# Splitting keys and queries on GpSimd, transposing attention sums on VectorE in 32 by 32 blocks, and padding earlier, in a fused attention and expert kernel

## What is computed

```python
scores = jnp.clip(jnp.einsum('bhqd,bhkd->bhqk', Q, K), -80.0, 80.0)
scores = jnp.where(causal, scores, -jnp.inf)
weights = jax.nn.softmax(scores / jnp.sqrt(jnp.float32(d_qk)), axis=-1)
attn = jnp.einsum('bhqk,bhkd->bhqd', weights, V)
x = _layernorm(x + attn.transpose(0, 2, 1, 3).reshape(B, S, 128) @ W_O)
top_idx = jnp.argmax(x @ gate_w.T + gate_b + expert_bias, axis=-1)
# out += (top_idx == e) * (relu(x @ w1[e] + b1[e]) @ w2[e] + b2[e])   for each expert e
x = _layernorm(x + out)
```

## Time and profile before

| | us |
|---|---|
| median of 3 runs | 439.85 (438.35 to 442.32) |
| the profiled execution | 439.83 |
| its span (first to last instruction) | 438.1 |
| mean granted TensorE clock | 0.982 of full |

### The profile page before, as it was taken

The page is one execution under the profiler, slowest core; times in us unless marked ns, Lnnn a source line. Parts: engine busy times, 40 slices in busy tenths (PEclk is TensorE's granted clock), DMA queues, the critical chain, the costliest instruction groups (busy, mean ns, idle before and its releaser), DMA issues. The chain is left out here.

```text
span 438.1 us, 12324 instructions
## 1 busy us (share of the span) xinstructions
PE 416.3 (95%) x4235; PEld 230.2 (53%) x4235; DVE 362.1 (83%) x824; ACT 356.4 (81%) x568; POOL 152.1 (35%) x164
## 2 busy tenths in 40 slices
PE   8899999999999999999999999998999899699993
PEld 6533344444443444444444444443444698599992
DVE  3978897999998889999987999999878578377764
ACT  3979999999998999998899999998889564376661
POOL 8221001315213013512401314212001466688887
PEclk9889999999999999999999999999899999899998
DMA  5268510668671135544500760674410255477640
GB/s 154 50 167 195 162 49 1 144 145 227 145 170 30 45 87 126 123 112 103 133 2 6 164 149 27 142 170 133 125 39 2 73 140 156 146 223 197 200 136 20
DMA packets 33005, 50.62 MB, mean 116 GB/s; under 512 B 5627, under 2 KB 16545, under 8 KB 32944
## 3 DMA queue, kind: packets, MB, share of 16 engines
q1 hardware_dynamic: 25488, 36.51, 34.1%
q10 hardware_dynamic: 5184, 9.05, 7.3%
q0 software_dynamic: 2272, 4.27, 2.9%
HBM read 21.35 MB, written 5.33 MB: 61 GB/s over the span
## 5 line engine op out<-in xcount | busy, mean ns | idle before, releaser
L1032 ACT ACTIVATE prob<-ring 128x1024 f32<-128x1024 f32 x288 | 274.5, 1039 | 25.8 <-PE ring L1224 25.0
L1242 PE MATMUL o_acc<-prob,v_stat 128*32 128x512 f32 (+3 forms) x1536 | 155.8, 501 | 2.9 <-DVE prob L705 2.1
L1224 PE MATMUL ring<-queries,keys 32*128 32x512 f32 (+3 forms) x1536 | 126.8, 385 | 0.4 <-DVE queries L665 0.4
L1224 PEld LDWEIGHTS ring<-queries,keys 32*128 32x128 f32 x1536 | 71.0, 187 | 71.4 <-issue 48.0
L691 DVE TENSOR_SCALAR prob<-prob 128x2048 f32<-128x2048 f32 x64 | 77.4, 1220 | 7.2 <-ACT prob L1032 6.8
L705 DVE SCALAR_TENSOR_TENSOR prob<-prob,mask_hi 128x1024 f32<-128x1024 f32 (+1 forms) x80 | 82.2, 1028 | 0.0
L1120 ACT ACTIVATE prob<-ring,b1T 128x128 f32<-128x128 f32 x156 | 44.6, 368 | 35.6 <-issue 16.4
L704 DVE TENSOR_SCALAR prob<-prob 128x1024 f32<-128x1024 f32 (+1 forms) x80 | 64.7, 808 | 6.6 <-ACT prob L1032 6.1
L584 POOL DMA_INDIRECT by_expert<-xrow,index x32 | 40.1, 1254 | 78.1 <-DVE index L800 71.0
L1242 PEld LDWEIGHTS o_acc<-prob,v_stat 128*32 128x32 f32 x1536 | 34.1, 109 | 57.2 <-issue 39.5
L565 POOL TENSOR_TENSOR rstd<-var_eps,const 128x4 f32<-128x4 f32 x8 | 16.4, 2048 | 92.0 <-DVE var_eps L748 92.0
(11 more groups left out here) (117 smaller groups left out, 343.5 us busy)
## 6 DMA issues: line engine op xcount, KB each, us to landing
queries<-query_parts SPq DMA_DIRECT2D x60, 256.0 KB, 4.0
v_stat<-in_w ACTq DMA_DIRECT2D x34, 256.0 KB
keys<-key_parts SPq DMA_DIRECT2D x60, 128.0 KB, 2.5
queries<-by_expert SPq DMA_DIRECT2D x39, 66.0 KB
xrow<-in_x_rows SPq DMA_DIRECT2D x8, 264.0 KB, 4.4
xT<-in_x_T SPq DMA_DIRECT2D x8, 256.0 KB, 3.0
v_stat<-in_w SPq DMA_DIRECT2D x5, 256.0 KB
out<-prob,queries POOLq DMA_INDIRECT x39
```

What stands on the lines that cost most here:

```text
L1032: act.activation(prob[u % P_SLOTS][:, 2 * half:2 * half + 2, :].rearrange("p h s -> p (h s)"), slot(("score", u, half))[:], ACT.Exp, scale ...
L1224: last = pe.matmul(out[:, j % 2 * QC + off:j % 2 * QC + off + w], keys[hg][r, kt * P:(kt + 1) * P], queries[hg][r, qc, part, QC - w:QC], s ...
L1242: last = pe.matmul(o_acc[j * VW:(j + 1) * VW, QC - w:QC], v_stat[b % 2][:, hg, kt, j, :], prob[u % P_SLOTS][:, j, off:off + w], start=begi ...
```

## The change

Four things are done together.

1. **GpSimd makes the lower parts.** `lower_of_keys` and `lower_of_queries` leave VectorE; `parts_of` on GpSimd runs the two casts and then the two subtractions. Project jobs of the own batch's second pair move from units 3 and 8 to 10 and 13.
2. **Sums are turned by VectorE.** The jobs "turn" and "flip" are gone from TensorE, and the flip's evacuation from ScalarE. VectorE transposes `o_sb` in 32 by 32 blocks (`turn_sum`), takes one reciprocal and one product per sum, and, for the second pair, transposes again (`attn_turned`). W_O's rows are reordered on loading to match. This happens right behind the clip of the unit in which ScalarE copies the sum (n = 7, 20, 25 and 2 of the next batch).
3. **Pads in the last batch.** SyncE lays 1152 padding rows (the most that the last batch and a tile can need) behind each region straight from DRAM to DRAM, eight DMAs of 608 KB, before the last batch's routes write over them. Those routes wait for `padded`. No pad is left in the expert loop.
4. **The early plan in four parts**, at units 23, 24, 27 and 28 of the last batch, and the tail's late jobs and plan one tile earlier.

```diff
-OWN_JOBS = {3: ("project", 1, 0), 8: ("project", 1, 1),
-            16: ("turn", 0, 0), 23: ("turn", 0, 1), 26: ("turn", 1, 0), 28: ("flip", 0), 29: ("out", 0),
-            33: ("turnx", 0), 34: ("gate", 0), 35: ("rank", 0)}
-LATE_JOBS = {4: ("turn", 1, 1), 6: ("flip", 1), 7: ("out", 1), 10: ("turnx", 1), 12: ("gate", 1), 14: ("rank", 1)}
-NEXT_JOBS = {18: ("latent", 0), 20: ("latent", 1), 24: ("v", 0), 25: ("project", 0, 0), 30: ("v", 1), 31: ("project", 0, 1)}
+OWN_JOBS = {10: ("project", 1, 0), 13: ("project", 1, 1), 29: ("out", 0), 33: ("turnx", 0), 34: ("gate", 0),
+            35: ("rank", 0)}
+LATE_JOBS = {7: ("out", 1), 11: ("turnx", 1), 12: ("gate", 1), 14: ("rank", 1)}
+NEXT_JOBS = {20: ("latent", 0), 25: ("latent", 1), 26: ("project", 0, 0), 27: ("v", 0), 30: ("v", 1),
+             31: ("project", 0, 1)}
-TAIL_AT = {1: "turn", 2: "flip", 3: "out", 6: "turnx", 7: "gate", 8: "rank"}
-PLAN_AT = (8, 9, 10)
-EARLY_PLAN_AT = (B - 1) * UB + 16
-ROUTE_AT = {9: (0, 1), 10: (2, 3)}
-PAD_AT = 9
-PADS_ACT = 2
+TAIL_AT = {2: "out", 5: "turnx", 6: "gate", 7: "rank"}
+PLAN_AT = (7, 8, 9)
+EARLY_PLAN_AT = (23, 24, 27, 28)
+ROUTE_AT = {8: (0, 1), 9: (2, 3)}
+PAD_ROWS = S + P
...
+                    for q in range(Q):
+                        sp.wait_ge(routed[q], b * QT * 16)
+                    sp.wait_ge(pad_ready, 1)
+                    for e in range(E):
+                        at = sp.value_load(pad_at[0:1, e:e + 1], min_val=0, max_val=DUMMY - PAD_ROWS)
+                        sp.dma_start(by_expert[bass.ds(at, PAD_ROWS), :], io["pad_rows"]).then_inc(padded, 16)
...
-            pad(sp, range(E - PADS_ACT))
...
+                pool.wait_ge(upper_keys, i + 1)
+                pool.tensor_tensor(key_parts[i % 2][:, 1, :], whole_k[i % 2][:], key_parts[i % 2][:, 0, :], ALU.subtract
+                                   ).then_inc(lower_keys, 1)
+                pool.wait_ge(upper_queries, i + 1)
+                pool.tensor_tensor(query_parts[i % 2][:, 1, :], whole_q[i % 2][:], query_parts[i % 2][:, 0, :], ALU.subtract
+                                   ).then_inc(lower_queries, 1)
...
+            def turn_sum(k):
+                dve.wait_ge(o_out, k + 1)
+                dve.transpose(flipped[k % NQC][:], o_sb[k % 2][:]).then_inc(o_turned, 1)
...
             def normalize(k):
...
+                dve.reciprocal(rsum[:], o[:, :, DH:2 * VS:VS]).then_inc(rsum_ready, 1)
                 dve.wait_ge(rsum_ready, k + 1)
...
+                if pair == PAIRS - 1:
+                    dve.wait_ge(attn_ready, k + 1)
+                    dve.transpose(flipped[qc][:], attn_blocks[qc][:]).then_inc(attn_turned, 1)
```

More of the change, by code:

```diff
@@ L96, in numbered @@
     kind, *which = job
-    if kind == "turn":
-        return kind, sums(b, *which)
     return (kind, b, *which) if kind in ("project", "direct") else (kind, b * NQC + which[0])
@@ L364, in taken @@
             i = which[0]
-            return {"turn": (attn_ready, i + 1), "flip": (flip_out, i + 1), "out": (added, i + 1),
+            return {"out": (added, i + 1),
                     "turnx": (turnx_out, i + 1), "gate": (logits_out, i + 1), "rank": (carried, i + 2),
@@ L590, in _ @@
                 if step_job(u, "project"):
[L591 removed]
+                    parts_of(*step_job(u, "project")[1:])
                 if route_at(u):
@@ L802, in job @@
             def job(kind, i):
-                if kind == "turn":
-                    normalize(i)
                 if kind == "out":
@@ L821, in before_clip @@
                     turn_queries(*which)
-                if kind == "turn":
-                    normalize(*which)
                 if kind == "out":
@@ L896, in _ @@
                 clip(u)
-                split = 0 if u == 0 else u - 1 if u > 1 else None
-                if split is not None and step_job(split, "project"):
-                    lower_of_keys(*step_job(split, "project")[1:])
-                    lower_of_queries(*step_job(split, "project")[1:])
+                if sum_ended(u) is not None:
+                    turn_sum(sum_ended(u))
                 if u == 20:
@@ L1257, in job @@
                 claim_misc((kind, i))
[L1258 to L1271 removed]
+                if kind == "out":
+                    pe.wait_ge(attn_turned, i + 1)
                     pe.wait_ge(out_w_in, 16)
@@ L1435, in key_query_weights, with output_weights @@
     return out
+def output_weights(a):
+    rows = a["L0_attn_W_O"].reshape(PAIRS, 2, HG, DH, D).transpose(2, 0, 1, 3, 4)
+    return np.ascontiguousarray(rows.reshape(HEADS * DH, D))
 def constants():
```

195 lines of the change are left out of this document (81 added, 114 removed).

## The result

The changed kernel takes **455.9 us** (median of 4 runs, 453.91 to 466.43) against 440.97 us of the kernel before beside it (438.35 to 442.32): a ratio of 1.0344, 95% interval 1.0291 to 1.0397. It is slower by 3.4%, where the prediction had 427 us and a range up to 441. One of the four runs, 466.43 us, was slow as a whole (clock 0.83 where the others have 0.96 to 0.97), and the ratio is made without it; the other three took 453.91 to 456.30 us.

The account below looks back on a forecast made before the run. TensorE was taken as the bound, VectorE and ScalarE at 92% right behind. 438.1 - 6.0 + 1.0 - 3.0 - 4.0 - 1.0 = 425.1 us of span, forecast 427 us, range 418 to 441.

Parts of the forecast that it names:

- part 3: Attention batches: GpSimd's subtractions, 1.2 us each, would hold VectorE 0.9 us in three of four cases, 5.4 us a batch.
- the period: Inner batch: VectorE's need of 78.5 us beside TensorE's 77.7, plus 2 us, gives 80.5 us; -6.0 us over 3.93 batches.
- rival (a): Attention batches: every subtraction holds a clip 1.0 us, VectorE needs 81.1 and becomes the bound; 437 us, chance 0.18.
- Rival (b): Attention batches: subtractions of 1.8 us each hold VectorE 1.6 us, its need 85.9, period 87; 452 us, chance 0.12.
- Parts 1 and 2: Attention batch: turns and flips gone save TensorE 3.5 us and ScalarE 1.3; VectorE's own work falls 2.1 us.
- the places: Project jobs moved within a batch: 1 to 2 us to spare for the longer chain, nothing booked.
- The start: First batch: keys just spread come later by about one subtraction, +1.0 us.
- Part 4: Last batch: the early plan in four parts removes 2.1 us of idle TensorE and 1.7 of clock; -3.0 booked.
- Part 5: Expert loop: pads moved out recover most of 5.5 us lost there, -4.0 booked; in the last batch they just fit.
- Part 6: Tail: its turn and flip leave TensorE, 2 x 0.65 us, and VectorE gains some 2 us; -1.0 booked.

Follow-up runs that it names:

- e1: The changed kernel with the lower parts of keys and queries made by VectorE again, GpSimd's subtractions gone: 431.5 us, 0.9834 of the kernel before.
- e3: The kernel before, with GpSimd also doing each lower-part subtraction (512 columns) into unread scratch while VectorE makes the real ones: 459.08 us, 1.0438.
- e10: The kernel before, with two more GpSimd casts of 128x512 per project into unread scratch: 440.96 us, 1.0056.
- e13: The kernel before, with two more GpSimd subtractions of 256 columns per project into unread scratch: 443.19 us, 1.0084.
- e15: The changed kernel with each GpSimd subtraction of 512 columns issued as two of 256: 443.38 us, 1.0083 of the kernel before.
- e8: e1 with the jobs back at the places of the kernel before: 437.58 us, 0.9955 of the kernel before.
- e7: e1 with the early plan in one piece at unit 16 of the last batch, as before: 431.85 us, 0.9836 of the kernel before.
- e14: The kernel before with only the early plan split in four, at units 18, 20, 22 and 24 of the last batch: 437.14 us, 0.9943.
- e6: e1 with the pads back in the expert loop, issued by SyncE and ScalarE, none in the last batch: 430.76 us, 0.9807 of the kernel before.
- e16: The changed kernel with GpSimd's subtractions halved and the next batch's second-keys project at unit 28 instead of 31: 453.99 us, 1.0300 of the kernel before.
- e2: The kernel before with only the lower parts moved to GpSimd, in its old order of jobs: 452.67 us, 1.0316.
- e4: The changed kernel with the next batch's second-keys project at unit 28 instead of 31: 444.33 us, 1.0109 of the kernel before.
- e5: e1 with the eight last routes spread, one behind each of tiles 1 to 4 and 8 to 11: 438.93 us, 0.9984 of the kernel before.

## Why the prediction was wrong, point by point

"Part" is here a part of the prediction. GpSimd's subtractions, point 1 of the change, are its part 3.

**The step that failed is part 3**, and with it the period. "A subtraction would cost 1.2 - 0.18 = 1.0 ... I take 0.9" was close for one meeting (1.08). "Not each one will meet a clip ... I take three in four" gave 5.4 us a batch, and that was too little: e1's VectorE shows 77.5 us, of which 5.4 are its own subtractions, so 72.1 without them, and the changed kernel shows 80.6 and 81.8. That is 8.5 and 9.7 us of waits, as if every subtraction held it for 1.1 to 1.2 us. VectorE's need was near the 81.1 of rival (a). Then "with two within a microsecond of each other ... I add 2 us: 80.5". This is what fell hardest. The batches took 85.8 and 88.7, so 5 to 7 us over VectorE's busy time. Adding up an engine's busy time treats a wait as if it could lie anywhere. But one project's two subtractions lie on a chain that TensorE waits for (power, layernorm, transpose), they hold it 2.45 us in each of the first three batches, and TensorE's clock often falls behind that. Of the 5.3 and 8.2 us that the inner batches lose to e1's, 3.3 and 3.9 are idle time of TensorE, and 1.9 and 4.2 are longer busy time for the same work at a lower clock (0.98 and 0.96 in the mean). The prediction had no term for the clock here. e1 shows the size of the mistake: 24.4 us by medians, 22.4 by the ratios, where the sum had the two sides cancel (5.4 us given up, 5.4 us of wait). e3, e10, e13 and e15 show that it is a matter of one instruction's length at that place.

**Rival (b)** was the right sign with the wrong premise: its time, 452 us, is 4 us from the result, but it wanted subtractions of 1.8 us and "about 1.2 us of wait for each" on VectorE's sum. The subtraction took 1.26 us alone, the wait was 1.08, and VectorE's busy time stayed under the 82.9 that it named as the point of decision. That it came near is partly luck: it adds 1 us to VectorE's 85.9, where (a) and the forecast add 2.

**Parts 1 and 2 and the period without the subtractions were right**, by e1: TensorE's need 78.1 (77.7), ScalarE's 74.1 (74.0), VectorE's 77.5 with its own subtractions (73.1 + 5.4 = 78.5), the period 80.53 (80.5). The match of the period is partly luck: the 80.5 was meant for VectorE at 78.5 and all subtractions on GpSimd. And the prediction booked the gain to the relief of TensorE and "nothing" to the places; e8 shows that the relief alone gives no gain and both together 1.5 us a batch.

**The start**, booked at +1.0: the wait is real, its price isn't to be told apart. TensorE's wait for the second keys is 1.92 us, where e1 has 0.28, so 1.6 us for "about one subtraction". But of two kernels that are the same up to there, e1 has a first batch of 78.65 us and e7 80.63, as TensorE is granted 1.00 and 0.69 of its clock from 17 to 22 us.

**Part 4** was right in the kernel before: 2.5 us by e14 for the 3.0 booked. In the surroundings of e1 the medians show 0.4 us of it (e7), though in e7's trace the old plan's stall does reach TensorE.

**Part 5 was wrong**: 4.0 us booked, nothing found (e6). The step was "SyncE issues six pads from 368.75 on ... and TensorE 2.20 us behind it", which took what stood next to the stall for its cause. Four routes stood there too (372.17 to 378.7), and in e1, without pads, the stall is there. The pads' own cost was rightly hidden: eight issues from 329.26 to 339.61, landed by 348.08, 18.8 us (16 to 21), and the first tile waits for no DMA.

**Part 6**, booked at -1.0: the loop from the last exponentials on takes 99.03 us in e1, 99.66 before, 0.6 less together with part 5.

In sum e1's four batches are 9.3 us shorter than those of the kernel before (periods 78.65, 80.53, 80.53 and 77.48 against 82.65, 81.95, 82.05 and 79.84), where 8.0 were booked (6.0 - 1.0 + 3.0), and its expert loop 0.6 us, where 5.0 were. That is nearly the whole of 428.4 against 425.1 us of span. Some 2 us of the first batch's 4.0 are luck, since e7 doesn't have them. The 25.4 us from there to 453.8 come with part 3. They lie in the four batches (about 7.4, 5.3, 8.2 and 2.4 us) and, with 2.2 us, in the expert loop, where no subtraction runs: there the longer second stall is what differs, and the cause of that stays open.

What beats both kernels is the change without the subtractions on GpSimd: e1 (431.5 us, 0.9834) or, with the pads left where they were, e6 (430.76 us, 0.9807).

## What to carry to other kernels

Price work moved to a neighbour by its longest single instruction and by the tightest chain that can meet it, not by its total against the engine's free time: 30 instructions of 0.61 us cost 2.8 us here, 30 of 1.3 us 19. And the fullest engine's clock is a term of its own: here it was about a third of an inner batch's loss in one case and half in the other. Look for the places where the fullest engine waits for a few small operations of VectorE or for a power on GpSimd, and keep long GpSimd instructions away from them, on its ports and in its queue; if the move must be made, cut a long one in two, and then look at the chain that the halves make longer (e15, e16). No kernel here with all subtractions on GpSimd, moved or halved, was as fast as the kernel before, so here they belong on VectorE. And when a stall has two suspects beside it, undo each alone before booking its gain.

## What the runs showed of the hardware that was not expected

- A stall of TensorE can cost more than twice its length, through the clock: the three units with the wait of 2.45 us took 5.4 us longer than in e1, at 0.66 of the clock for 10 us. Behind 2.16 us (e16) it was 0.66 too, behind 1.34 us (e15) 1.00. But equal waits are followed by different clocks: 2.45 us by 0.83, 0.83 and 0.66 in the changed kernel, 2.47 us by 0.83, 1.00 and 1.00 in e2, e4's pairs once by 0.63 and twice by 1.00. So the length alone doesn't decide, and no run here shows what does. In e6 two waits of 1.08 and 1.53 us near tile 12 left the clock at 1.00, where e1's one wait of 1.88 us had 0.69 behind it (371 to 376.5 us).
- GpSimd is held in turn, and longer than it holds: a cast of 0.61 us took 3.88 us at 209.09 us of the changed kernel, beside four clips of VectorE that each took their usual time; a subtraction's mean was 1.56 and 1.64 us for 1.26 alone.
- Very small operations of VectorE pay the whole wait: the sum of 128x32 (L770), 0.19 us alone, took 1.18 once.
- Two subtractions of 256 columns take 0.73 us each, where one of 512 takes 1.26: halving costs 0.2 us a subtraction.
- ScalarE's first issue of weights in the expert loop takes 2.27 us (336.37 in e1), 0.35 for most others. It takes 0.9 to 1.1 us in every kernel that has the expert loop of the kernel before (1.07 there, at 345.12), and 2.2 to 2.7 in every one with the changed loop, with and without routes beside it (e5) or pads ahead of it (e6); no run here shows why.
